# A three-stage mixture-of-experts kernel: the third norm taken on rows, slots counted by a running sum, and the gathers of the third stage issued in the middle of a step

## Time and profile before

| | before |
|---|---|
| runs, median (range) | 3320.6 us (3319.63 to 3323.88) |
| profiled execution | 3318.28 us |
| its span, first to last instruction | 3316.4 us |
| mean granted TensorE clock | 0.901 of full speed |
| busy: PE, PE weight load | 2775.0 us (84%), 2181.5 us (66%) |
| busy: DVE, ACT, POOL | 1901.2 us (57%), 1843.2 us (56%), 1134.6 us (34%) |

### The profile page before, as it was taken

The page is one execution under the profiler, slowest core; times in us unless marked ns, Lnnn a source line. Parts: engine busy times, 40 slices in busy tenths (PEclk is TensorE's granted clock), DMA queues, the critical chain, the costliest instruction groups (busy, mean ns, idle before and its releaser), DMA issues.

```text
span 3316.4 us, 69976 instructions
## 1 busy us (share of the span) xinstructions
PE 2775.0 (84%) x25687; PEld 2181.5 (66%) x25687; DVE 1901.2 (57%) x4527; ACT 1843.2 (56%) x3725; POOL 1134.6 (34%) x964
## 2 busy tenths in 40 slices
PE   6999999999999859999996677877788777877787
PEld 4766666666666549999995456655566555655565
DVE  4878878878788742222221355655565555655566
ACT  4777777777777734444443345544454444544454
POOL 1454555655555530000002533333333333333310
PEclk9999999999999979999998688887888888878888
DMA  3222222222222137777774111111111111111110
GB/s 119 88 84 72 96 83 72 101 78 75 100 76 73 42 114 228 228 230 227 230 228 140 34 40 41 29 41 44 44 40 27 43 44 43 40 28 44 44 30 26
DMA packets 139758, 287.14 MB, mean 87 GB/s; under 512 B 25440, under 2 KB 82784, under 8 KB 135392
## 3 DMA queue, kind: packets, MB, share of 16 engines
q1 hardware_dynamic: 114912, 245.68, 22.9%
q0 software_dynamic: 24576, 37.80, 4.2%
HBM read 215.08 MB, written 68.29 MB: 85 GB/s over the span
## 4 chain that ended last, share of the span: by engine, by line
PE 47%; issue 7%; another core or an unknown queue 4%; DVE 3%; ACT 1%; POOL 1%; DMA 0%; SPq 0%; DVEq 0%; ACTq 0%; POOLq 0%
PE psum L1174 8%; PE psum L1165 8%; PE psum L1538 7%; PE psum L1498 5%; PE psum L1555 3%; PE psum L1568 3%; PE psum L1523 2%; PE psum L1503 2%; PE psum L1580 2%; DVE qdiag L1837 1%; PE psum L1598 1%; PE psum L1156 1%; PE psum L1546 1%; DVE inv L1852 1%
## 5 line engine op out<-in xcount | busy, mean ns | idle before, releaser
L1466 POOL DMA_INDIRECT ycho<-expert_out,place x384 | 367.5, 957 | 1417.4 <-DVE place L1829 1309.7
L1208 ACT ACTIVATE hid<-psum,w_blk 128x256 f32<-128x256 f32 x608 | 269.1, 474 | 326.2 <-PE psum L1165 326.2
L1039 POOL DMA_INDIRECT expert_in<-rows,slot_i x384 | 392.3, 1022 | 133.2 <-issue 111.6
L1852 DVE RECIPROCAL inv<-psum 128x64 f32<-128x64 f32 x288 | 159.5, 554 | 464.7 <-remote 385.9
L1538 PE MATMUL psum<-keys,qdiag 64*64 64x80 f32 x4608 | 281.4, 256 | 124.1 <-issue 123.7
L1752 ACT ACTIVATE ex<-psum,smin 128x80 f32<-128x80 f32 x1152 | 282.2, 332 | 142.9 <-DVE smin L1845 135.8
L1538 PEld LDWEIGHTS psum<-keys,qdiag 64*64 64x64 f32 x4608 | 214.8, 148 | 211.1 <-issue 195.7
L502 PE MATMUL psum<-xn,w_in 128*128 128x288 f32 x1024 | 311.1, 429 | 39.6 <-DVE xn L861 10.2
L1174 PE MATMUL psum<-w_blk,hid 128*128 128x128 f32 x2432 | 296.6, 275 | 0.0
L1568 PE MATMUL psum<-ex_t,pair_ones 128*32 128x64 f32 x4608 | 137.8, 244 | 189.6 <-DVE half L1853 124.0
L1165 PE MATMUL psum<-x_t,w_blk 128*128 128x256 f32 x1216 | 289.5, 381 | 2.4 <-DMA w_blk<-w_exp_in 2.4
(11 more groups left out here) (247 smaller groups left out, 5848.5 us busy)
## 6 DMA issues: line engine op xcount, KB each, us to landing
w_blk<-w_exp_in SPq DMA_DIRECT2D x152, 578.0 KB, 3.8
xin<-x_in SPq DMA_DIRECT2D x32, 1716.0 KB
rows_in<-expert_in SPq DMA_DIRECT2D x152, 128.0 KB, 2.3
expert_out<-rows_out SPq DMA_DIRECT2D x152, 128.0 KB, 3.0
h_dram<-h SPq DMA_DIRECT2D x32, 288.0 KB
x_dram<-x SPq DMA_DIRECT2D x32, 288.0 KB
h1c<-h_dram SPq DMA_DIRECT2D x32, 288.0 KB
x2c<-x_dram SPq DMA_DIRECT2D x32, 288.0 KB
```

The lines of the kernel that those rows point to most:

```text
L1039: pool.indirect_dma_start(out=expert_in[:, :], out_offset=bass.IndirectOffsetOnAxis(ap=slot_i[z.s][:, n:n + 1], axis=0), in_=rows[z.s][:, ...
L1208: nc.scalar.activation(hid[b.s][:, c, :], HB[b.s][c % HK], ACT.Gelu_apprx_tanh, bias=w_blk[b.q][:, FF + FC * D + c:FF + FC * D + c + 1]).t ...
L1466: pool.indirect_dma_start(out=ycho[x.s][:, k, :], out_offset=None, in_=expert_out[:, :], in_offset=bass.IndirectOffsetOnAxis(ap=place[x.s] ...
L1852: v.reciprocal(inv[:], sum_bank()).then_inc(head_step, 1)
```

## The change

- Stage A: `picks` is stored expert-major; a running sum over the groups (`upto_g`, one tensor_tensor_scan with a 0/1 mask that restarts it for each expert) replaces `newly`. "before" becomes the triangular matrix minus ones, so that ranks need three products instead of seven. `chosen` takes the last group of the running sum. ranks wait for route step 15 (the scan) instead of 13.
- Stage A: x2 is stored to DRAM from `rows` (96 partitions x 3072 B) instead of from the feature tile (128 x 2304 B); the wait for that store goes from DVE, ahead of x2, to ACT, ahead of the copy at L741. The gelu table is loaded once ahead of the loop instead of once a step.
- Between B and C: one more product of one column, and two tiny DVE operations.
- Stage C: x2 comes in the row layout and POOL adds it (three adds and multiplies instead of two). Layer norm 3 is made on rows: DVE statistics of each row (six bn_stats, six bn_aggr, one small product), ACT a small Ln and Exp and six ACTIVATEs of 96x128, all for w. The six PE transposes are of the normed rows, for w, in bank A1 where the product with "center" stood. The products with "center" and "mean" for norm 3, the square, Ln and Exp over 128x576, prec and x3 are gone; h2 comes from PSUM in one operation.
- Stage C: the gathers of v additionally wait until PE has issued the scores of x's fourth unit.

```diff
-        "before": (p[:, None] < p[None, :])[:, :G],
+        "before": (p[:, None] < p[None, :])[:, :G] - 1.0,
...
-                    hold(sp, x2_step, z.upto(2, 2))
-                    sp.dma_start(x2_dram[:, a_range(z.n, z.s)], x2[z.s][:]).then_inc(x2_stored[z.s], 16)
+                    hold(sp, rows_ready, z.upto(2, 2))
+                    sp.dma_start(x2_dram[row_range(z.n, z.s), :], rows[z.s][:].rearrange("p g d -> p (g d)")
+                                 ).then_inc(x2_stored[z.s], 16)
...
-                pe.wait_ge(route_step, z.upto(ROUTE, 13))
+                pe.wait_ge(route_step, z.upto(ROUTE, 15))
...
-                nc.tensor.matmul(dst, C("before")[0:G, :], picks[z.s][:], start=True, stop=False)
-                for g in range(NG - 1):
-                    nc.tensor.matmul(dst[:, g + 1:NG, :], C("ones")[0:G, 0:G],
-                                     picks[z.s][:, g:g + 1, :].to_broadcast([G, NG - 1 - g, E]),
-                                     start=False, stop=False)
+                nc.tensor.matmul(dst, C("before")[0:G, :], by_group(picks[z.s][:]), start=True, stop=False)
+                nc.tensor.matmul(dst, C("ones")[0:G, 0:G], by_group(upto_g[z.s][:]), start=False, stop=False)
...
             act.wait_ge(consts_ready, 4)
+            act.preload_act_table_set("gelu_apprx_tanh_and_others")
...
-                act.preload_act_table_set("gelu_apprx_tanh_and_others")
...
                         act.wait_ge(scattered[z.s], 16 * 2 * NG * z.n)
+                        act.wait_ge(x2_stored[z.s], 16 * z.n)
...
-            v.tensor_reduce(newly[s][:], picks[s][:].rearrange("p g e -> p e g"), AX_X, ALU.add
-                            ).then_inc(route_step, 1)
+            v.tensor_tensor_scan(upto_g[s][:], within[:], picks[s][:], 0.0, ALU.mult, ALU.add).then_inc(route_step, 1)
...
-            def gather(x):
+            def gather(x, during):
                 hold(pool, place_ready, x.upto(1, 1))
+                if during:
+                    hold(pool, scores_done, during.upto(NU, 4))
                 if x.old(2):
-                    hold(pool, moe_done, x.upto(1, -1))
+                    hold(pool, ysum_step, x.upto(YSUM, -YSUM))
...
+                pool.wait_ge(x2_landed[x.s], 16 * x.n + 16)
+                pool.wait_ge(ysum_step, x.upto(YSUM, 1))
+                pool.tensor_tensor(x2c[x.s][:], x2c[x.s][:], ycho[x.s][:, 0:NG, :], ALU.add).then_inc(ysum_step, 1)
+                pool.wait_ge(ysum_step, x.upto(YSUM, 2))
                 if x.old(1):
-                    pool.wait_ge(moe_done, x.upto(1, 0))
-                pool.tensor_tensor(ysum[:], ycho[x.s][:, 0:NG, :], ycho[x.s][:, NG:, :], ALU.add
-                                   ).then_inc(ysum_step, 1)
+                    pool.wait_ge(nrows_ready, x.upto(1, 0))
+                pool.tensor_tensor(ysum[:], x2c[x.s][:], ycho[x.s][:, NG:, :], ALU.add).then_inc(ysum_step, 1)
...
                 if v:
-                    gather(v)
+                    gather(v, x)
                     weighted_sum(v)
...
             def moe(x, bank):
-                pe.wait_ge(ysum_step, x.upto(2, 2))
+                pe.wait_ge(nrows_ready, x.upto(1, 1))
...
-                    pe.wait_ge(prec_ready, w.upto(1, 1))
-                    project(A1, C("center"), prec[:]).then_inc(norm3_pe, 1)
+                    moe(w, A1)
...
-                    pe.wait_ge(norm3_act, w.upto(3, 1))
-                    project(A0, C("mean"), sq3[:]).then_inc(norm3_pe, 1)
...
-                if v:
-                    if w:
-                        pe.wait_ge(norm4_act, w.upto(3, 2))
-                    elif v.old(1):
-                        pe.wait_ge(prec_ready, v.upto(1, 0))
-                    moe(v, A0)
...
+            def row_root(x):
+                act.wait_ge(stats_ready, x.upto(1, 1))
+                nc.scalar.activation(root3[:], stats[:, :, 1], ACT.Ln, bias=eps_col[0:G, 0:1]).then_inc(root_step, 1)
+                act.wait_ge(root_step, x.upto(2, 1))
+                nc.scalar.activation(root3[:], root3[:], ACT.Exp, scale=-0.5).then_inc(root_step, 1)
+
+            def normed_rows(x):
+                act.wait_ge(moved_ready, x.upto(1, 1))
+                if x.old(1):
+                    act.wait_ge(moe_done, x.upto(1, 0))
+                for g in range(NG):
+                    last = nc.scalar.activation(nrows[:, g, :], ysum[:, g, :], ACT.Identity, bias=move3[:, g:g + 1],
+                                                scale=root3[:, g:g + 1])
+                last.then_inc(nrows_ready, 1)
...
                     exps(x, 1)
+                if w:
+                    row_root(w)
+                if x:
                     turned(x, 0)
...
                     turned(x, 1)
                     exps(x, 2)
+                if w:
+                    normed_rows(w)
                 if y:
                     inverse_root(y, r5, A0, norm5_pe, norm5_act)
...
-                if w:
-                    square(w, sq3, A1, norm3_pe, norm3_act)
...
+            def row_halves(x):
+
+                v.wait_ge(ysum_step, x.upto(YSUM, YSUM))
+                for g in range(NG):
+                    last = v.bn_stats(halves3[:, g, :], ysum[:, g, :])
+                last.then_inc(halves3_ready, 1)
...
                 if z:
                     pick_gate(v, z)
+                if w:
+                    row_halves(w)
                 if y:
                     halves(y, 8)
                     heads(y, 8)
+                if w:
+                    row_stats(w)
                 if x:
                     minimum(x, 1)
...
                     minimum(x, 2)
+                if w:
+                    row_moves(w)
...
-                if w:
-                    v.wait_ge(moe_done, w.upto(1, 1))
-                    v.wait_ge(h_landed[w.s], 32 * w.n + 32)
-                    v.tensor_tensor(two(prec[:]), both(A0), two(x2c[w.s][:]), ALU.add).then_inc(prec_ready, 1)
...
-                    v.wait_ge(norm3_act, w.upto(3, 3))
-                    v.scalar_tensor_tensor(out=two(x3[:]), in0=both(A1), scalar=V("ln3_g"), in1=two(r3[:]),
-                                           op0=ALU.mult, op1=ALU.mult).then_inc(x3_ready, 1)
+                    v.wait_ge(moe_done, w.upto(1, 1))
+                    v.wait_ge(h_landed[w.s], 16 * w.n + 16)
+                    v.scalar_tensor_tensor(out=two(h2[:, w.s * T:(w.s + 1) * T]), in0=both(A1), scalar=V("ln3_g"),
+                                           in1=two(h1c[w.s][:]), op0=ALU.mult, op1=ALU.add).then_inc(h2_ready, 1)
```

More of the change, by code:

```diff
@@ L223, in build @@
         consts_ready = sem("consts_ready")
-        held = {"sync": sem("held_sync"), "pool": sem("held_pool"), "tensor": sem("held_tensor")}
+        held = {"sync": sem("held_sync"), "pool": sem("held_pool"), "tensor": sem("held_tensor"),
+                "vector": sem("held_vector")}
         def first(n):
@@ L400, in a_prep_vector @@
             step(v.memset(chosen[:], 0.0))
+            step(v.memset(within[:], 1.0))
+            settle()
+            step(v.memset(by_group(within[:])[:, 0, :], 0.0))
             for s in range(2):
@@ L1425, in load @@
                 sp.dma_start(h1c[x.s][:], h1_dram[:, a_range(x.n, x.s)]).then_inc(h_landed[x.s], 16)
-                sp.dma_start(x2c[x.s][:], x2_dram[:, a_range(x.n, x.s)]).then_inc(h_landed[x.s], 16)
+                if x.old(2):
+                    hold(sp, ysum_step, x.upto(YSUM, -YSUM))
+                sp.dma_start(x2c[x.s][:].rearrange("p g d -> p (g d)"), x2_dram[row_range(x.n, x.s), :]
+                             ).then_inc(x2_landed[x.s], 16)
             def experts(x):
@@ L1714, in c_scalar, with square @@
             act.wait_ge(zeroed, 1)
-            def square(x, dst, bank, pe_done, done):
+            def square(x, dst, bank, pe_done, done, **bias):
                 act.wait_ge(pe_done, x.upto(2, 1))
-                nc.scalar.activation(two(dst[:]), both(bank), ACT.Square).then_inc(done, 1)
+                nc.scalar.activation(two(dst[:]), both(bank), ACT.Square, **bias).then_inc(done, 1)
+            def row_root(x):
[11 more added lines that the diff above has]
+                last.then_inc(nrows_ready, 1)
             def inverse_root(x, dst, bank, pe_done, done):
@@ L1806, in step @@
                 if w:
-                    square(w, sq4, A1, norm4_pe, norm4_act)
+                    square(w, sq4, A1, norm4_pe, norm4_act, bias=shift3[:, 0:1])
                 if x:
@@ L1861, in heads, with row_stats, row_moves @@
                                 one_head[:], inv[:], ALU.mult).then_inc(att_ready, 1)
+            def row_halves(x):
[3 more added lines that the diff above has]
+                last.then_inc(halves3_ready, 1)
+            def row_stats(x):
+                v.wait_ge(halves3_ready, x.upto(1, 1))
+                if x.old(1):
+                    v.wait_ge(moved_ready, x.upto(1, 0))
+                for g in range(NG):
```

(12 more changed lines are left out.)

62 lines of the change are left out of this document (28 added, 34 removed).

## The result

The changed kernel takes 3327.47 us (median of 20 runs, 3322.13 to 3331.43) where the kernel before takes 3320.39 (20 runs): a ratio of 1.0021, 95% interval 1.0014 to 1.0028. It is slower by 0.2%. Forecast was 3277 us, 1.3% faster; 3327 lies inside the range of 3105 to 3350, but on the other side of no change, by 7.1 us: hardly more than the 6.6 us that the prediction counted as no change (chance 0.11), and just inside what it called slower (0.19).

What follows compares the result with a forecast made beforehand. TensorE was taken to bound stage A, and waits for gathers, about 14.9 us a step, to be stage C's largest item. 3318.3 - 34 (norm 3) - 10 (ranks) + 0.5 = 3274.8, 3277 us on the median's scale; whole range 3105 to 3350.

Steps and rivals of the forecast that it cites:

- The reading of the stall: Stage C: with indirect DMAs in flight TensorE passes some 5 matmuls a microsecond, wherever they fall; only small ones suffer.
- Norm 3 on rows: Stage C: layer norm 3 on rows nets -1.1 us a step, bounds -2.2 to +1.6; -34 us over 31 steps.
- two products: Stage C, norm 3: two products of four records each leave TensorE, 1.03 and 1.17 us, -2.2 us a step.
- at 0.28 each: Stage C, ScalarE: six row ACTIVATEs take 1.7 us (1.2 to 2.2), of which about 1.1 shows as TensorE wait.
- I take 0 from it and keep 1.7: Stage C: VectorE's added row work, ahead of a minimum that exps wait for, costs 0, with 1.7 us as bound.
- VectorE's own term: Stage C: six bn_stats, six bn_aggr and one product take VectorE 3.2 us; it loses 1.5 us elsewhere.
- The place: Stage C: gathers moved to the middle of a step gain 0, near bounds +0.6 and -3.5 us a step.
- rival (a): Stage C: the middle covers the hand-offs, saving 3.5 us a step, 105 more, 3172 us; chance 0.20.
- Ranks: Stage A: three products instead of seven, less a later start, net -0.3 us in 32 steps, -10 us (-20 to 0).
- (b): Stage C: the middle is the worse place for gathers, +1.8 us a step, +46 us, 3366 us; chance 0.11.
- (c): Stage C: POOL's three sums hold VectorE's operations, +2.2 us a step, 3379 us, at half 3328; chance 0.08.
- (d): Nothing measurable: the transposes' wait for rows and xm eats the 2.2 us; 3311 us, 3320 without ranks; chance 0.09.

Runs made afterwards that it cites:

- e11: Kernel before with gathers of all items but the first two left out and POOL's two sums held until the fourth scores: 2866 us, a step of 31.4 us.
- e4: Kernel after with the gathers of all items but the first two left out: 2894 us, a step of 32.3 us.
- e3: Kernel after with its 12 gathers a step in six bursts of two, behind the 1st to 6th scores: 3181.82 us, ratio 0.958.
- e8: Kernel after with each of the 12 gathers held on its own behind 12 successive posts of TensorE: 3131.57 us, ratio 0.9433.
- e1: Kernel after with the gathers issued at the head of a step as before, not after the fourth scores: 3343.05 us, ratio 1.0063.
- e6: Kernel after with norm 5's inverse root ahead of the six row ACTIVATEs on ScalarE: 3329.02 us, ratio 1.0032.
- e7: Kernel after with the six row operations on VectorE instead of ScalarE, ahead of xm: 3329.19 us, ratio 1.0033.
- e10: Kernel before, norm 3 by products, with its gathers held one by one as in e8: 3093.77 us, ratio 0.9281.
- e5: Kernel before with the gathers of all items but the first two left out: 2972 us, a step of 34.8 us.
- e13: e4 with the six row operations on VectorE instead of ScalarE: 3024 us, a step of 36.8 us.
- e14: Kernel after with only the first six gathers of each item from the third item on: 3069.55 us, a step of 38.3 us.
- e15: Kernel before with gathers one by one as in e10, plus stage A's slots by running sum with one table load: 3091.09 us, ratio 0.9262.

## Why the prediction was wrong

**What bounds stage C** was right: the stall of the gathers, 14.9 us a step by the tail, 14.9 by e11 in the kernel before and 14.3 by e4 in the kernel after.

**The reading of the stall** ("wherever they fall", "large matmuls don't notice") was right in its total and wrong in its form. Some 80 to 90 matmuls do pass in any window of 12 gathers, but not at an even rate: 63 in 6 us, then 17 in 11. In the slow part one matmul takes 0.7 us, VectorE gets what it waits for 11 us late, and the clock falls to half and stays there for 4 to 8 us behind it. From the even rate it followed that spreading is worth nothing; e3 and e8 show that it is worth 4 and 6%. One reading of the earlier trace rows was off as well: of "the 7 to 9 us waits ending with the landing" none does. The waits of 7.23 and 9.12 us end at 2721.18 and 2723.26, in the middle of the burst; only the one of 6.09 us ends behind the landing.

**Norm 3 on rows, -1.1 us a step, is the step that failed**: e4 and e11 have it at +0.9, from 1.6 us less work and 2.5 us of new waits. Its terms:

- *"two products ... -2.2 us a step"*. TensorE's busy time fell by 1.6 us a step (e11 against e4).
- *"at 0.28 each ... 1.7 us ... about 1.1 shows"*. The six ACTIVATEs keep ScalarE busy for 2.42 us a step, past the bound of 2.2. The wait that the term was for, the transposes' for xm, came out near: 1.35 us.
- *What was put at nothing.* "h2 and xq keep their places with about the same operands: 0" and "The six transposes are made either way" leave out that the transposes had been filling the time of xq: 0.48 us a step. For exps (0.36) and heads (0.32) there was a bound, "I take 0 from it and keep 1.7". Together 1.16 us, the largest part of the 2.0 us between forecast and outcome. e11 shows that TensorE did not wait at all before; so every new wait costs in full. I took the path as limited by TensorE and then priced one wait, when the chain around it had no spare time.

VectorE's own term was priced too high: the statistics keep it busy for 1.9 us a step (32.2 + 13.0 + 3.9 us in 26 steps), not 3.2. The outcome of +0.9 lies inside the bounds of -2.2 to +1.6; the value in them was wrong, and with it the direction.

Over 31 steps +0.9 and -1.1 are 62 us apart. The miss is 50 us, with the 14 us that the place won against it 64: the rest of the sum is small. With the gathers at the head of a step the row path makes it longer by 1.4 us from 1900 to 2900 us, by 1.25 over all steps (e1).

**The place, 0 with +0.6 and -3.5 as bounds**, measured -0.7 us a step over all steps (46.95 to 46.22) and 14 us by the ratios; the 23 us of the steps hold the scatter of two profiled runs. Right in its bounds. Whether it is the covering of hand-offs, rival (a), at a seventh to a fifth of its price, or something else, is not shown: the place also moves POOL's sums from VectorE's gdiag to its att (below). That the window may swallow what is early in it was not seen; it would be why e6 and e7 gain nothing.

**Ranks, -10 us**: the first block of stage B starts at 1208.6 us instead of 1216.6. But among the profiles with stage A unchanged it starts at 1208.1 (e11), 1212.1 (e10), 1216.6 (before) and 1219.4 (e5), and among the 15 with the new one at 1204.2 (e13) to 1212.8 (e6), 1208.7 on average against 1214.1. So some 5 us are likely, and 8 are not shown. Ranks, table load and x2's store can't be told apart in it.

**The parts by e1**: rows and stage A +21 us, the place -14, +7 in all. Since e1 is the only run between the two kernels, this sum closes by itself and checks nothing.

**The rivals.** (b), a worse place, is refuted: the middle is the better one. (c) has a part in it, but its two sides cancel. In the kernel after POOL's sums run beside att, which takes 0.367 us instead of 0.284 (+0.75 us a step on VectorE), and no longer beside gdiag, 0.218 instead of 1.327 (-1.1):

```profile
L1880 DVE TENSOR_TENSOR att<-one_head,inv 128x64 f32<-128x64 f32 x233 | 85.6, 367 | 8.1
L2030 DVE TENSOR_SCALAR gdiag<-cst,g 4x4 f32<-4x4 f32 x26 | 5.7, 218 | 0.9
```

Where the sums fall on more of VectorE's work its full price shows (e13, e5). (d) came nearest, with 3311 to 3320 us and a chance of 0.09. Its mechanism, "the transposes' wait for rows and xm eats the 2.2 us", holds for 1.35 us of the 2.5.

**Left open:** what slows TensorE and its posts while gathers are in flight; no run tells more than that it goes with the burst. Why bursts of four are dearest. And which operation of the row path makes the waits for exps and heads, 0.68 us a step.

## What to carry to other kernels

Ask, before work is taken off the busiest engine, whether that engine has any idle time at all when the known stall is gone: if it is busy 100%, every operation that the replacement puts in a chain of hand-offs costs in full. A stall that is bound to an event (a burst of gathers) should first be tried in other shapes: held one at a time behind 12 posts, which made bursts of one to four, it gained 7% in the kernel before, where shifting the whole burst gained 0.4% in the kernel with rows. An operation that is made either way can still be filling a gap where it stands. And a price read from a smaller operation was a lower bound here: 0.28 against 0.40 us busy and 0.50 from start to end.

## What the runs showed of the hardware

- While POOL's indirect DMAs are issued without a break, what the other engines wait for from TensorE comes late: VectorE waited up to 13.4 us behind 12 gathers, 5.2 behind six (e14), 4 to 5 behind four and up to 3.6 where most bursts were of two (e3). The DMA engines are busy only 0.14 of that stretch, which speaks against a contention for data; no run tests it. The Trainium skill (SBUF — State Buffer, Who interferes with whom) says that a DMA never contends with a compute engine and that TensorE never waits on anyone. For its ports that may hold; for its progress the trace disagrees: 17 matmuls in 11.3 us, with gaps of up to 1.8 us for which the profile shows nothing that it waited for.
- Bursts of four are worse than one of twelve (48.7 against 46.6 us a step), the mixtures of e3 and e8 better (42.0, 40.2). In e15 the granted clock from 2000 to 2800 us is 0.96, in the kernel after 0.83.
- In the two steps shown above the clock came back 4 us (before) and 8 us (after) behind the landing, and TensorE worked at half speed for most of that time: it was busy 3.86 of 4.3 us and 6.49 of 7.0.
- Six ACTIVATEs of 96x128 with a bias and a scale from tiles keep ScalarE busy for 2.42 us, 0.40 each, though one takes 0.499 from start to end.
